# Attention's maxima written straight into a shift operand, one of them ahead of the routing, and projections as single fp32 matmuls

## The reference

```python
x = x + 0.5 * ffn(layernorm(x))      # mixture of experts, then a layer norm of x + out
x = x + attn(layernorm(x))
x = x + 0.5 * ffn(layernorm(x))      # the same weights again
```

```python
q = rope(x @ w_q.T);  k = rope(x @ w_k.T);  v = x @ w_v.T
y = softmax(q @ k.T / sqrt(8)) @ v       # per batch and head, 256 x 256 scores
out = y @ w_o.T
```

## Time and profile before

| | |
|---|---|
| median of 3 runs | 499.18 us (498.59 to 502.23) |
| profiled execution, first to last instruction | 468.6 us |
| PE busy | 398.1 us, 85% |
| DVE busy | 354.2 us, 76% |
| ACT busy | 256.6 us, 55% |
| POOL busy | 209.3 us, 45% |
| mean granted TensorE clock | 0.924 of 2.4 GHz |
| head, to | about 54 us |
| first expert phase | 54 to 168 us |
| attention | 168 to about 340 us |
| second expert phase and end | to 468.6 us |
| one batch in the middle of attention (L1498 at 251.39, 274.70) | 23.3 us |

### The profile page before, as it was taken

The page is one execution under the profiler, slowest core; times in us unless marked ns, Lnnn a source line. Parts: engine busy times, 40 slices in busy tenths (PEclk is TensorE's granted clock), DMA queues, the critical chain, the costliest instruction groups (busy, mean ns, idle before and its releaser), DMA issues. The chain is left out here.

```text
span 468.6 us, 10269 instructions
## 1 busy us (share of the span) xinstructions
PE 398.1 (85%) x3166; PEld 318.9 (68%) x3166; DVE 354.2 (76%) x1149; ACT 256.6 (55%) x518; POOL 209.3 (45%) x269
## 2 busy tenths in 40 slices
PE   5847698998999989989898989899999899999800
PEld 4533488997898856766665666676578799998700
DVE  5688374657887788899999999976547865569845
ACT  1423266766557563767474757576486466666400
POOL 5284775884554311120204242515136768445521
PEclk9776699999999995999999999999799999999955
DMA  9710642223111119940000000001201222232231
GB/s 279 282 47 30 176 142 68 58 58 103 43 49 29 32 52 335 322 157 23 1 24 13 13 13 13 25 6 37 51 18 58 65 73 58 58 103 86 69 112 45
DMA packets 33203, 37.81 MB, mean 81 GB/s; under 512 B 5504, under 2 KB 28032, under 8 KB 32752
## 3 DMA queue, kind: packets, MB, share of 16 engines
q1 hardware_dynamic: 28144, 27.36, 19.4%
q0 software_dynamic: 4544, 9.35, 5.9%
q10 hardware_dynamic: 464, 0.44, 0.4%
HBM read 26.71 MB, written 20.36 MB: 100 GB/s over the span
## 5 line engine op out<-in xcount | busy, mean ns | idle before, releaser
L1247 ACT ACTIVATE stage<-ps 128x512 f32<-128x512 f32 x78 | 46.6, 598 | 66.6 <-PE ps L768 66.5
L1839 DVE TENSOR_REDUCE mx<-ps 128x4 f32<-128x1024 f32 x64 | 77.2, 1213 | 6.2 <-PE ps L888 6.1
L1303 ACT ACTIVATE stage<-ps 128x1024 f32<-128x1024 f32 x64 | 65.5, 1023 | 27.4 <-PE ps L899 26.6
L793 PE MATMUL ps<-w_hl,ring_hi 128*128 x234 | 64.3, 344 | 1.4 <-DVE stage L1733 1.4
L1725 DVE TENSOR_TENSOR ring_hi<-ps,ring_hi 128x512 fp32r<-128x512 f32 x78 | 53.8, 689 | 14.1 <-ACT ring_hi L1254 13.7
L502 POOL DMA_INDIRECT sorted_x<-rows,place_at x32 | 31.9, 997 | 67.0 <-DVE place_at L1543 56.1
L1719 DVE TENSOR_TENSOR bx<-ps,bx 128x128 fp32r<-128x128 f32 x78 | 22.4, 288 | 50.6 <-ACT bx L1229 48.4
L794 PE MATMUL ps<-w_hl,ring_hi 128*128 x312 | 60.6, 235 | 0.0
L521 POOL DMA_INDIRECT expert_y<-stage x39 | 38.9, 998 | 41.0 <-DVE stage L1733 38.9
L794 PEld LDWEIGHTS ps<-w_hl,ring_hi 128*128 128x128 f32 x312 | 54.0, 191 | 0.0
L521 POOL DMA_INDIRECT expert_y<-stage,arena x39 | 38.6, 991 | 33.1 <-DVE stage L1733 29.4
(11 more groups left out here) (204 smaller groups left out, 1024.4 us busy)
## 6 DMA issues: line engine op xcount, KB each, us to landing
sorted_x<-fill SPq DMA_DIRECT2D x8, 1096.5 KB, 18.3
stage<-w SPq DMA_DIRECT2D x16, 256.0 KB, 6.3
y_got<-expert_y SPq DMA_DIRECT2D x24, 128.0 KB, 2.3
stage<-sorted_x SPq DMA_DIRECT2D x39, 64.5 KB, 1.8
arena<-sorted_x SPq DMA_DIRECT2D x39, 64.5 KB, 1.8
x_tok<-x SPq DMA_DIRECT2D x4, 256.0 KB, 5.0
sorted_x<-rows,place_at POOLq DMA_INDIRECT x64, 2.4
stage<-sel SPq DMA_DIRECT2D x1, 1024.0 KB
```

The costliest lines, as they stand in the source:

```text
L793: pe.matmul(both, bg_hi[:, s, c, :], w, start=(c == 0), stop=False, skip_group_check=True)
L1247: act.activation(g_full[:, s, :], ps[:, H_BANK, :], ACT.Gelu).then_inc(g_done, 1)
L1303: act.activation(prob[:, 2 * v:2 * v + 2, :], ps[:, at:at + 2, :], ACT.Exp, scale=SCALE)\
L1839: vec.tensor_reduce(mx[:, t, :].rearrange("p (r g j) -> p r j g", r=2, g=2)[:, pair, 2 * jp:2 * jp + 2, :], ps[:, at:at + 2, :].rearrange( ...
```

## The change

`ident_r` becomes `minus_eye_r`, the negated identity, so that the matmul of `place_shifted` brings in the sign. `maxima` writes directly to column 24 of `shift` (rounded to fp32r); `mx`, both `negate` and the semaphore `shift_ready` go, and `place_shifted` waits for `max_done`. Maximum 6 of each batch moves on DVE from behind the sums of `combine` to right behind `rotate_sin`, ahead of `gating`. `project`, `values` and `project_out` use one fp32 matmul where they had three fp32r ones, so `wa_hi`, `wa_lo`, `split_wa`, `low_wa`, `a_low_x` and `low_y` go; ACT's copies write fp32 and release PE directly. Before `placing` DVE waits for `yt_ready`, now ACT's copy of y. The weights of attention are loaded straight into their own tile. In the first phase `qk` waits for the load, and the first `place` for the two splits of `sel`.

```diff
-        ident_r = sb("ident_r", [P, P], F32R)
+        minus_eye_r = sb("minus_eye_r", [P, P], F32R)
-        wa_hi = sb("wa_hi", [P, 6, P], F32R)
-        wa_lo = sb("wa_lo", [P, 6, P], F32R)
+        wa = sb("wa", [P, 6, P])
...
-            sp.dma_start(wa_raw, watt).then_inc(att_loaded, 16)
+            sp.dma_start(wa[:, :, :].rearrange("p a m -> p (a m)"), watt).then_inc(att_loaded, 16)
...
             def project(p, first_w, bank):
                 for m in range(2):
-                    mm = pass3(ps[:, bank, m * SEQ:(m + 1) * SEQ], wa_hi[:, first_w + m, :], wa_lo[:, first_w + m, :],
-                               ax_hi[:, p, :], ax_lo[:, p, :])
+                    mm = pe.matmul(ps[:, bank, m * SEQ:(m + 1) * SEQ], wa[:, first_w + m, :], ax[:, p, :],
+                                   start=True, stop=True)
...
             def qk(b, p, bank=M1):
-                pe.wait_ge(a_xlo_done, b + 1)
+                pe.wait_ge(ax_ready, b + 1)
...
-                    mm = pass3(ps[:, bank, rows], ax_hi[:, p, rows], ax_lo[:, p, rows], wa_hi[:, 4, :], wa_lo[:, 4, :])
+                    mm = pe.matmul(ps[:, bank, rows], ax[:, p, rows], wa[:, 4, :], start=True, stop=True)
...
             def place_shifted(b, p, pair, bank=M0):
-                pe.wait_ge(shift_ready, 2 * b + pair + 1)
+                pe.wait_ge(max_done, SU * b + 4 * pair + 4 + MAX_BUF)
...
-                                       shift[:, t * 512 + g * P:t * 512 + (g + 1) * P], ident_r[:, :],
+                                       shift[:, t * 512 + g * P:t * 512 + (g + 1) * P], minus_eye_r[:, :],
...
             def project_out(b, bank=M0):
-                    mm = pass3(ps[:, bank, rows], yt_hi[:, rows], yt_lo[:, rows], wa_hi[:, 5, :], wa_lo[:, 5, :])
+                    mm = pe.matmul(ps[:, bank, rows], yt[:, rows], wa[:, 5, :], start=True, stop=True)
...
             def beside_first(s):        # PE
                 if s == 29:
-                    pe.wait_ge(att_split, 4)
+                    pe.wait_ge(att_loaded, 32)
                     qk(0, 0, M0)
                 if s == 32:
                     qk_swapped(1, 1, M0)
+                    pe.wait_ge(att_split, 2)
                     place(0, 0, 0, M1)
...
             def a_copy_x(b, p):         # ACT
-                act.activation(ax_hi[:, p, :], ps[:, M1, 0:SEQ], ACT.Copy).then_inc(a_xhi_done, 1)
+                act.activation(ax[:, p, :], ps[:, M1, 0:SEQ], ACT.Copy).then_inc(ax_ready, 1)
             def copy_y(b, bank=M0):
-                act.activation(yt_hi, ps[:, bank, 0:SEQ], ACT.Copy).then_inc(ythi_done, 1)
+                act.activation(yt[:, :], ps[:, bank, 0:SEQ], ACT.Copy).then_inc(yt_ready, 1)
...
             def maxima(b, *us):         # DVE
-                        mx[:, t, :].rearrange("p (r g j) -> p r j g", r=2, g=2)[:, pair, 2 * jp:2 * jp + 2, :],
+                        shift_v[:, t, :, 24].rearrange("p (r g j) -> p r j g", r=2, g=2)[:, pair, 2 * jp:2 * jp + 2, :],
...
             def batch(b, p, tail=True, place_next=True, project_next=True, norm=True):   # DVE
                 if place_next:
                     maxima(b + 1, 3)
-                    negate(b + 1, 0)
-                if project_next:
-                    a_low_x(b + 2, p)
-                if tail:
-                    low_y(b - 1)
                 if b >= 3 and place_next:
+                    vec.wait_ge(yt_ready, b)
                     placing(FIRST_UNIT + b - 3)
...
                 if project_next:
                     rotate_sin(b + 2, p)
+                if place_next:
+                    maxima(b + 1, 6)
                 if b >= 2:
                     gating(FIRST_UNIT + b - 2)
                     add_chosen(FIRST_UNIT + b - 2)
                 if norm:
                     combine(b + 3, apply_part=False)
-                if place_next:
-                    maxima(b + 1, 6)
                 if norm:
                     combine(b + 3, sum_part=False)
...
                 if place_next:
                     maxima(b + 1, 7)
-                    negate(b + 1, 1)
```

More of the change, by code:

```diff
@@ L225, in build @@
         prstd = sb("prstd", [P, 2, BT])
-        mx = sb("mx", [P, BT, HEADS])
         rden = sb("rden", [P, HEADS])
@@ L241, in build @@
         arena = sb("arena", [P, 4864])
-        ring_lo = sb("ring_lo", [P, 2560], F32R)
-        x_hi = sb("x_hi", [P, 1536], F32R)
-        x_lo = sb("x_lo", [P, 1536], F32R)
+        ring_lo = sb("ring_lo", [P, 2048], F32R)
+        rot_hi = sb("rot_hi", [P, 2, 2, SEQ], F32R)
+        rot_lo = sb("rot_lo", [P, 2, 2, SEQ], F32R)
+        ax = sb("ax", [P, 2, SEQ])
+        yt = sb("yt", [P, SEQ])
         w_raw = stage[:, :].rearrange("p (a e n) -> p a e n", a=2, e=EXPERTS)
@@ L250, in build @@
         sel_raw = stage[:, 4096:6144]
-        wa_raw = stage[:, 6144:6912]
         y_end = stage[:, 4096:6144].rearrange("p (b k t d) -> p b k t d", b=BATCH // 2, k=PICKS, t=BT)
@@ L266, in build @@
         qk4 = ring_hi[:, :].rearrange("p (s g m n) -> p s g m n", s=2, g=HG, m=2)
[L267 to L270, removed]
         qs4 = ring_lo[:, 0:1024].rearrange("p (g n) -> p g n", g=HG)
@@ L273, in build @@
         shift_v = shift.rearrange("p (t h c) -> p t h c", t=BT, h=HEADS)
-        yt_hi = ring_lo[:, 2048:2304]
-        yt_lo = ring_lo[:, 2304:2560]
         v4 = arena[:, 0:2048].rearrange("p (s t h c) -> p s t h c", s=2, t=BT, h=HEADS)
@@ L317, in build @@
         att_split, shift_zeroed, ones_set = sem("att_split"), sem("shift_zeroed"), sem("ones_set")
-        a_ln_done, a_xt_filled, a_xhi_done, a_xlo_done = (
-            sem("a_ln_done"), sem("a_xt_filled"), sem("a_xhi_done"), sem("a_xlo_done"))
+        a_ln_done, a_xt_filled, ax_ready = sem("a_ln_done"), sem("a_xt_filled"), sem("ax_ready")
         qk_filled, cos_done, qks_filled, sin_done, rot_ready = (
@@ L322, in build @@
         v_filled, v_ready, sel_filled, qk4_ready = sem("v_filled"), sem("v_ready"), sem("sel_filled"), sem("qk4_ready")
-        s_filled, max_done, shift_ready = sem("s_filled"), sem("max_done"), sem("shift_ready")
+        s_filled, max_done = sem("s_filled"), sem("max_done")
         qs_filled, qs_ready = sem("qs_filled"), sem("qs_ready")
@@ L326, in build @@
         pv_filled, y4_ready, yq_filled, y_ready = sem("pv_filled"), sem("y4_ready"), sem("yq_filled"), sem("y_ready")
-        yt_filled, ythi_done, yt_ready, o_filled, att_done = (
-            sem("yt_filled"), sem("ythi_done"), sem("yt_ready"), sem("o_filled"), sem("att_done"))
+        yt_filled, yt_ready, o_filled, att_done = (
+            sem("yt_filled"), sem("yt_ready"), sem("o_filled"), sem("att_done"))
         stored = sem("stored")
@@ L641, in _ @@
             expert_regs = [pe.alloc_register(f"pe_expert{i}") for i in range(4)]
[L643 to L647, removed]
             def keep_busy(bank, many):
@@ L1357, in split_sel @@
                                sel_raw[:, 1024 * half:1024 * half + 1024], ACT.Copy).then_inc(att_split, 1)
-            def split_wa():
-                act.wait_ge(att_loaded, 32)
-                act.activation(wa_hi[:, :, :].rearrange("p a m -> p (a m)"), wa_raw, ACT.Copy).then_inc(att_split, 1)
             def beside_first(s):
@@ L1371, in beside_first @@
                     split_sel(1)
-                if s == 11:
-                    split_wa()
                 if s == 28:
@@ L1679, in head @@
                 vec.wait_ge(b_loaded, 48)
-                vec.tensor_copy(ident_r[:, :], ident).then_inc(const_split, 1)
+                vec.tensor_scalar(minus_eye_r[:, :], ident, -1.0, None, ALU.mult).then_inc(const_split, 1)
                 vec.tensor_copy(tri_r[:, :], tri_raw).then_inc(const_split, 1)
@@ L1750, in blocks @@
                         beside_second(s)
-            def low_wa():
-                vec.wait_ge(att_split, 3)
-                vec.tensor_tensor(wa_lo[:, :, :].rearrange("p a m -> p (a m)"), wa_raw,
-                                  wa_hi[:, :, :].rearrange("p a m -> p (a m)").bitcast(F32), ALU.subtract)\
-                    .then_inc(att_split, 1)
             def combine(i, sum_part=True, apply_part=True, stats_part=None):
@@ L1810, in a_norm @@
                         .then_inc(a_ln_done, 1)
-            def a_low_x(b, p):
-                vec.wait_ge(a_xhi_done, b + 1)
-                vec.tensor_tensor(ax_lo[:, p, :], ps[:, M1, 0:SEQ], ax_hi[:, p, :].bitcast(F32),
-                                  ALU.subtract).then_inc(a_xlo_done, 1)
             def rotate_cos(b, bank=M1):
@@ L1860, in divide @@
                                   ALU.mult).then_inc(y_ready, 1)
-            def low_y(b, bank=M0):
-                vec.wait_ge(ythi_done, b + 1)
-                vec.tensor_tensor(yt_lo, ps[:, bank, 0:SEQ], yt_hi.bitcast(F32), ALU.subtract).then_inc(yt_ready, 1)
             def add_attention(b, bank=M0):
@@ L1946, in beside_first @@
                     shares(0)
-                if s == 12:
-                    low_wa()
```

(10 more changed lines are left out.)

4 lines of the change are left out of this document (removed).

## The result

| kernel | median, us | before, same chip and series | ratio, 95% interval |
|---|---|---|---|
| changed, first comparison | 493.19 | 500.83 | 0.984, 0.982 to 0.987 |
| changed, second (after_again) | 489.88 | 498.38 | 0.980, 0.975 to 0.985 |
| changed, third (after_third) | 463.48 | 468.09 | 0.989, 0.985 to 0.993 |

A series is a set of kernels run together on one chip. By medians the gain is 7.6, 8.5 and 4.6 us, by the ratios 8.0, 10.1 and 5.3; an execution that took over 1.5% longer than the fastest of its kernel is left out of the ratios, and the profile of after_again is of one such. The first comparison lies in the forecast's range (490.5 to 503.5) and outside the likeliest case's own (493.5 to 499) by a little; the second, 489.88, lies under the range. All three intervals exclude "no change", and by medians the gain is over 1% in the first two and just under it in the third.

The account below looks back on a forecast made before the run. DVE was taken to pace mid-attention with PE near, PE and ACT batch 6, PE the expert blocks. Terms 0.55 + 0.5 - 1.3 - 0.6 - 0.65 - 0.95 - 0.6 = -3.05 us took 499.18 to 496.2; range 490.5 to 503.5.

Parts of the forecast that it names:

- the likeliest case: Whole kernel: the summed terms hold, forecast 496.2 us, with 493.5 to 499 from their bounds; chance 0.45.
- the clock stays up: Rival, batches 0 and 7: PE's stretches at half clock vanish; 493.5 us with one, 490.7 with both; chance 0.28.
- my own sign of being wrong: PE's clock: a stretch at 0.50 in batches 1 to 4, or none in batch 0 or 7, would show the forecast wrong.
- the signs of being right: No low x, low y or sign on DVE; `gap` 0.16; waits of 1.05 (DVE) and 1.4 (step 1); batch 22.9 to 23.0.
- Batches 1 to 5, the middle: DVE after maximum 3: sign, low x and low y go, 0.9 us of slots, 0.45 won per batch (0.35 to 0.9).
- qk_swapped in fp32: PE during DVE's maximum 5: +0.2 us of projection, 0.13 more waiting on DVE per batch (0 to 0.3).
- Maximum 6: DVE ahead of routing: `gap` loses 1.03 us, but a wait for GpSimd's power appears; +0.05 in batches 0 to 4.
- that rival: DVE beside GpSimd's subtract: maximum 6 is held, +1.0 us in batches 0 to 5, 502 us in all; chance 0.07.
- The first expert phase: Ahead of attention: four 256-column projections +0.8, `values` -0.25, splitting the weights counts nothing; +0.55 us.
- Batch 0: At half clock two projections cost +0.4 us each and low x returns 0.3; +0.5 us.
- Batch 5: Attention without a combine: 0.35 from the middle and 0.25 from `values`; -0.6 us.
- batch 7 and the stretch behind: PE's wait for low y goes and its projections shorten, -0.95 us; low y and projection behind attention, -0.6.

Follow-up runs that it names:

- x_only: The kernel before with x alone projected by single fp32 matmuls, without low x on VectorE; 469.71 us for 469.13, ratio 1.001.
- six_only: The kernel before with maximum 6 moved ahead of the routing and nothing else; 497.75 us for 498.38, ratio 0.998.
- sign_only: The kernel before with the maxima's sign made on TensorE by a minus identity, nothing else; 500.69 us for 498.38, ratio 1.006.
- y_single: The kernel before with y alone projected by one fp32 matmul, without low y on VectorE; 463.03 us for 468.09, ratio 0.989.
- y_fill: y_single with four more filler matmuls in batch 0, where PE waits for the normalised x; 492.60 us for the kernel before's 501.98, ratio 0.984.
- before_fill: The kernel before with two more filler matmuls in batch 7, where PE waits for low y; 499.71 us for 501.98, ratio 0.9955.
- proj_again: The kernel before with both projections as single fp32 matmuls, no other part of the change, run once more; 462.60 us for 468.09, ratio 0.988.
- before_again: The kernel before, unchanged, profiled once more; 467.23 us, span 465.4.
- six_proj: The changed kernel with the sign put back on VectorE: maximum 6 ahead of the routing and fp32 projections; 464.53 us for 469.13, ratio 0.989.

## Why the prediction was right in its direction and short in its size

**The step that failed is a weight, not a term.** The rival "the clock stays up" had its place (PE's 0.56 us of waiting for low y in batch 7), its price (2.5 us) and the reason, and I gave it 0.28 and the forecast 0.45. At the lower level it is what happened, and my own sign of being wrong, no stretch at 0.50 in batch 7, came with it. Among the signs of being right, those on DVE, on `gap`, on the two waits and on the length of a batch all came. That the first comparison, 493.19, lies next to this rival's 493.5 is luck: the kernel before took 500.83 beside it and not 499.18, and 7.6 us were won where the rival has 5.5. The same place in the changed kernel (after_third) has neither the wait nor the fall, and `weigh` takes 1.93 us (timeline of PE, table of stretches):

```profile
329.40 0.51 PE L663 MATMUL ps<-const,x_t 128*128 128x8 f32 x4
329.77 0.69 PE L977 MATMUL ps<-wa,yt 128*128 128x128 f32 x4
...
332.43 1.93 PE L955 MATMUL ps<-stage,arena 128*32 128x256 f32 x32
```

```profile
329.50:341.00 11.50, 10.34 (x109) 6.79 (x108) 5.01 (x34) 8.34 (x16) 1.30 (x4) 1.00 0.19 47
```

Over all profiles: the five with that wait (two of before, x_only, six_only, sign_only) have a stretch at 1.2 GHz that begins within 2.5 us of it. Of the nine without it (four with both projections and more, y_single, y_fill, before_fill and the two of both projections alone) eight have none there. The ninth is proj_again, where the clock fell at 326.6 with PE waiting for nothing at the projection:

```profile
326.45 1.05 PE L978 MATMUL ps<-wa,yt 128*128 128x128 f32 x4
...
330.06 3.58 PE L956 MATMUL ps<-stage,arena 128*32 128x256 f32 x32
```

```profile
326.60:333.40 6.80, 6.80 (x46) 3.48 (x46) 3.42 (x24) 2.15 (x3) 1.07 (x3) 0.50 0.33 77
```

It is also the measure of the price: 33.25 us for 30.63 in the last column, 2.6, where the earlier trace rows had given 2.5. The profile of proj_again had the lowest clock of its six executions (0.928, the others 0.933 to 0.940), so this fall isn't its rule. In before_again the clock fell 0.2 us after the wait had begun (granted 1.00 from 329.75 to 329.95, 0.50 behind that), at nearly the same distance from maximum 5 of batch 6 as in proj_again (16.6 and 16.2 us), so in that execution it might have fallen without the wait. And at the upper level all seven profiles have one more stretch, of 3.4 or 6.8 us, between batch 6 and this place, with the wait and without it. So the wait makes the fall likely and isn't its only condition; before_fill, with its ratio and its lower time at 1.2 GHz, shows that it is a cause.

**Batches 1 to 5, the middle.** Forecast 0.45 for sign, low x and low y. From maximum 3 to maximum 4 before_again takes 243.11 - 240.40 = 2.71 us, after_third 244.25 - 241.88 = 2.37: 0.34 won. The row of `placing` says why not more, in the timelines of DVE and of ACT of after_third, and then in DVE's of y_single, which still has the sign and low x:

```profile
241.88 1.22 DVE L1808 TENSOR_REDUCE ring_lo<-ps 128x4 fp32r<-128x1024 f32 x1
243.66 0.19 DVE L1512 TENSOR_TENSOR ranks<-picks,ps 128x32 f32<-128x32 f32 x1 [0.56 <-ACT yt L1299]
...
244.25 1.22 DVE L1808 TENSOR_REDUCE ring_lo<-ps 128x4 fp32r<-128x1024 f32 x1
```

```profile
242.66 0.38 ACT L1174 ACTIVATE x_t<-ps 128x256 f32<-128x256 f32 x1
242.95 0.38 ACT L1266 ACTIVATE ax<-ps 128x256 f32<-128x256 f32 x1
243.24 0.39 ACT L1299 ACTIVATE yt<-ps 128x256 f32<-128x256 f32 x1
```

```profile
239.21 1.22 DVE L1839 TENSOR_REDUCE mx<-ps 128x4 f32<-128x1024 f32 x1
240.46 0.18 DVE L1847 TENSOR_SCALAR ring_lo<-mx 128x16 fp32r<-128x16 f32 x1
240.69 0.42 DVE L1814 TENSOR_TENSOR x_lo<-ps,x_hi 128x256 fp32r<-128x256 f32 x1
241.03 0.18 DVE L1532 TENSOR_TENSOR ranks<-picks,ps 128x32 f32<-128x32 f32 x1
...
241.60 1.22 DVE L1839 TENSOR_REDUCE mx<-ps 128x4 f32<-128x1024 f32 x1
```

The copy of y is ACT's third in a row, and DVE now idles 0.56 us for it. y_single does the sign and low x in that time and is no later (2.39). Of the three operations only one was worth its slot; the other two are paid out as waiting, which is why x_only (2.69) and sign_only (2.72) gave nothing there.

**The other terms in batches.** qk_swapped in fp32: from maximum 5 to the sine's product 1.31 us (247.09 to 248.40) for 1.14 (245.96 to 247.10), +0.17, forecast 0.13. The two matmuls of `qk` take PE 0.96 us from their start to that of the next instruction (291.13 to 292.09) where the six passes took 0.85 (290.49 to 291.34), +0.11 (timelines of PE, before_again, then after_third):

```profile
290.49 0.33 PE L645 MATMUL ps<-x_hi,wa_hi 128*128 128x256 f32 x1
...
291.34 0.38 PE L899 MATMUL ps<-ring_lo,ring_hi 32*128 32x256 f32 x2
```

```profile
291.13 1.03 PE L839 MATMUL ps<-ax,wa 128*128 128x256 f32 x4
292.09 0.38 PE L884 MATMUL ps<-ring_lo,ring_hi 32*128 32x256 f32 x2
```

For `qk_swapped` the record behind begins inside the last of its own, so I read to the second record behind: 1.09 (293.31 to 294.40) for 0.92 (292.63 to 293.55), +0.17. Forecast was +0.2 for each. `project_out` takes 0.52 (244.51 to 245.03) for 0.70, -0.18 and not -0.25. Maximum 6: `gap` takes 0.16 in every batch, and the wait that was to replace the stall is there, 1.14 us at DVE's first use of the statistics, behind GpSimd's power, where 1.07 had been forecast (timelines of DVE and of POOL, after_third):

```profile
250.19 1.22 DVE L1808 TENSOR_REDUCE ring_lo<-ps 128x4 fp32r<-128x1024 f32 x1
...
251.60 0.16 DVE L1478 TENSOR_TENSOR gap<-top 128x2 f32<-128x2 f32 x1
...
255.00 0.15 DVE L1761 BATCH_NORM_AGGREGATE pmv<-pstats 128x2 f32<-128x6 f32 x1
256.29 0.61 DVE L1768 SCALAR_TENSOR_TENSOR y_got<-y_got,pmv,const 128x128 f32<-128x128 f32 x2 [1.14 <-issue]
```

```profile
250.36 1.28 POOL L508 TENSOR_TENSOR rot_lo<-arena,rot_hi 128x512 fp32r<-128x512 f32 x1 [1.84 <-DVE rot_hi L1801]
...
255.50 0.69 POOL L469 TENSOR_TENSOR prstd<-prstd,neg_half 128x2 f32<-128x2 f32 x1
```

The profile names "issue" as the releaser, but the power ends at 255.50 + 0.69 = 256.19, 0.1 before DVE goes on. The maximum beside GpSimd's subtract takes 1.22, not held, so that rival falls. The rule quoted for it (the Trainium skill, SBUF — State Buffer, Who interferes with whom) agrees with this row. PE's scores at step 0 wait 0.24 us for nothing that the profile names, where they waited over 1 us for maximum 6, and those at step 1 wait 1.24 (forecast 1.4):

```profile
282.56 0.38 PE L884 MATMUL ps<-ring_lo,ring_hi 32*128 32x256 f32 x2 [1.24 <-DVE ring_lo L1808]
```

A batch comes to 23.03, forecast 22.9 to 23.0.

**Where terms were too large.** The first expert phase was to lose 0.55 and lost nothing (101.2 us both times); that its projections lie beside blocks with room for them is an inference. Batch 0 was to lose 0.5; its two periods gained 0.33, its stretch at 1.2 GHz being 6.8 us for 10.2. That gain isn't steady: with 6.8 us too, the two periods are 41.4 here, 40.5 in proj_again and 40.1 in six_proj. Batch 5 was to gain 0.6 and gained 0.16, batch 6 0.65 and 0.34. For batch 7 and the stretch behind, 1.55 us had been summed, at an unchanged clock; proj_again, whose clock fell there too, shows 0.86. So the terms alone come to 2.6 us for 3.05, close in part because their errors cancel, and the clock's 2.6 is on top.

The sum over the table is -5.2 us at the lower level. At the upper level the change gave -7.6 and -8.5 by medians.

**What stays open** is where the upper level's further 3 us come from; the intervals (0.982 to 0.987, and 0.985 to 0.993) overlap, so it may be less. What the profiles show of it: behind batch 6 the two kernels with the old projection have 10.2 us at 1.2 GHz (3.4 and 6.8) and take 40.5 and 39.9 us to the first block, the changed one has 6.8 and takes 37.3 and 39.1. In the second phase they have 17.0 and 13.6 us at that clock, the changed one 10.2 and 13.6, but its blocks took no less time. The clocks of all runs point the same way: the time at 1.2 GHz fell by 7 us at the lower level (67 to 60) and by 18 at the upper (100 to 82, after_again), which at half clock is worth at most 3.5 and 9 us, an estimate. Which waits these further stretches hang on was not tested. What sets the level of a series was not found. The engines wait in it for nothing that the profile shows, with the same instructions, DMA packets and bytes.

## What to carry to other kernels

Before adding up an operation's slot, ask which of the other engines is late next: three operations left DVE's middle here, and only the time to the copy of y on ACT was to be had. Where a short wait of PE stands right at the beginning of a stretch at half clock, removing the wait can be worth the stretch, several times the wait; a filler in its place tests that for the price of a line, and the mean clocks of all runs say more than one profile. Try each part alone, too: here the single matmul for y gave what the whole change gave. And compare a profile's own time with the times of the runs: if they differ by more than a few us, they are not the same kind of execution, and stages are to be compared only within one kind.

## What the runs showed of the hardware

At 2.4 GHz two fp32 matmuls with 256 moving columns took PE 0.96 us where the six fp32r passes in their place took 0.85; with 128 columns it was 0.52 for 0.70 (after_third and before_again). So one fp32 matmul was the dearer at 256 columns and the cheaper at 128. One chip ran the same kernel, the one before, at 498 us in one series and at 469 in the next, so the level is not the chip's; two others gave 468 and 502. It has 100 us of the span at 1.2 GHz in the upper level and 67 in the lower (twice the missing clock times the span: 2 x 0.101 x 496.0 and 2 x 0.072 x 466.3).
